# Bf16 instead of f32 integers in a SmoothQuant block: GpSimd clips in two passes and casts, TensorE transposes bf16, ScalarE copies without an offset

## The chip, the cores and the metric

One NeuronCore of a Trainium2 chip runs the whole kernel. The metric is the device time of one execution in microseconds. The kernel before takes 864.1 us (median of 3 runs, 863.93 to 864.49).

## The reference, cut to what matters

A decoder layer for 4 sequences of 512 tokens and 512 features: linear attention with 16 heads (x1 = layernorm(x + attention)), a quantised expert (x2 = layernorm(x1 + expert(x1))), and a gated FFN with 1408 hidden features and 4-bit weights (out = layernorm(x2 + ffn(x2))). The change lies in the expert, which calls this function twice, first with 512 input features (x and gate-up weights), then with 256 (the gated activation `a` and the down weights `v`):

```
def _smooth_quant_linear(x, w):
    ...                                   # s: per-feature smoothing from the column maxima
    xs = x / s
    ws = w * s
    x_scale = max(max|xs| over a row, EPS) / 127
    w_scale = max(max|ws| over a row, EPS) / 127
    x_q = jnp.clip(jnp.round(xs / x_scale), -127, 127)
    w_q = jnp.clip(jnp.round(ws / w_scale), -127, 127)
    return x_q @ w_q.T * x_scale * w_scale.T
```

## The kernel before, in words

Three phases follow one another, each a block in which every engine runs its own program and engines wait for each other through semaphores; a block ends when all its engines have ended.

1. `attention_phase` (0 to about 355 us): 16 chunks of 128 tokens. TensorE (PE) projects q, k and v with float32r matmuls, transposes q and k, forms scores and outputs. GpSimd (POOL) rotates q and k for the next chunk (L882 to L890), decays the state (L901, L910) and sums squares (L912, L914). ScalarE (ACT) and VectorE (DVE) drain PSUM. Beside the chunks, at places written out by hand in `EXPERT0_STEPS` as (chunk, part), run the steps of the expert for batch 0.
2. `weight_phase` (about 355 to 390 us): the 4-bit weights of the FFN are scaled into float32r.
3. `ffn_phase` (390 us to the end): for each of 4 batches, 11 hidden tiles of 128 features. A tile is on PE `hidden` for the gate (12 matmuls, L1476), `hidden` for up (12, L1476) and `down` of the tile before (12, L1486). After each of these three groups, at place 3*tile + 0, 1 or 2, PE runs the expert steps that `EXPERT_STEPS` puts there, for the next batch. ACT and DVE place their steps by the same table between their own parts of the tile; POOL has nothing else in this phase and runs the expert steps in order, as soon as their semaphores allow. Batches 1 to 3 of the expert run here, batch 3 of the FFN has none beside it.

The quantising of a matrix goes through these steps (names as in the two tables):

- `round_x`, `round_w`, `round_a`, `round_v` on ACT (L217): four instructions, one for each 128 rows, `src*inv + ROUND` with ROUND = 1.5 * 2^23, so that the f32 sum holds the rounded integer in its low bits. Each raises `rounded`.
- `clip_x`, `clip_w`, `clip_a`, `clip_v` on POOL (L279): two instructions, each for two of the four row blocks (128x1024 elements in the first layer, 128x512 in the second), min and max in one pass, in place, f32. Each raises `clipped`.
- `xq01`, `xq23`, `wq01`, `wq23`, `aq`, `vq` on PE (`quantised`, L467): for each of two feature blocks, four transposes of 128x128 f32 into one PSUM bank (6 or 7, in turn). The first feature block of a matrix waits for `clipped`, row blocks 0 and 1 for the first raise, 2 and 3 for the second. Before it writes a bank, PE waits until the bank's last user has drained it.
- the same names on ACT (`integers_out`, L223): the bank less ROUND, as bf16, into `q1T` or `q2T`.
- `w_scale`, `v_scale` (L456 on PE) broadcast a row of scales through the next bank; `products01` and so on (L476) multiply the bf16 integers; `rescale` (L392) on DVE; for the second layer `add` on POOL (L290), `sum` on DVE, `normalise` on ACT.

SyncE loads the next w once the bank of `vq1` is full, and the next v once that of `wq3` is full.

In PE's order an FFN batch has `xq01` at place 11, `xq23` 12, `wq01` 13, `wq23` 14, `w_scale` 15, then products, the second layer's columns at 19, rows at 21, `aq` 25, `vq` and `v_scale` 26, `y01` 27. In the attention, `xq01` and `xq23` are in chunk 8, `wq01` and `wq23` in chunk 9, `aq` and `vq` in chunk 14.

Of the kernel before, what the change touches and what calls it, by code (L numbers as in the profile page):

```python
# [7 lines left out]
ALU = mybir.AluOpType  # L8
# [142 lines left out]
class Expert:  # L151

    def __init__(self, nc, sem, memory):
# [4 lines left out]
            memory[n] for n in ("scale_row", "small", "e_stats", "e_mv", "biases"))  # L158
        self.v = self.w[:, :, 0:HALF]
        self.ps = memory["ps"]  # L160
        self.w_in, self.v_in, self.x1_in = sem("w_in"), sem("v_in"), sem("x1_in")
# [5 lines left out]
        self.inv_ready, self.rounded, self.clipped = sem("inv_ready"), sem("rounded"), sem("clipped")  # L167
        self.silu_g, self.e_var, self.e_root = sem("silu_g"), sem("e_var"), sem("e_root")
        self.gated, self.summed = sem("gated"), sem("summed")
        self.x2_shift, self.x2_done, self.mom = sem("x2_shift"), sem("x2_done"), sem("e_moments")  # L170
# [30 lines left out]
    def scalar_steps(self, act):  # L201
        nc, w, v, xb, act_s, q1T, q2T = self.nc, self.w, self.v, self.xb, self.act_s, self.q1T, self.q2T
        scale_row, small, mv = self.scale_row, self.small, self.mv
        ln_eps, plus_round, minus_round = (self.biases[:, n:n + 1] for n in (0, 2, 3))

# [14 lines left out]
        def integers_out(b, use, dst):  # L220

            self.wait_full(act, b, use)
            nc.scalar.activation(dst, self.bank(use)[:, :], ACT.Identity, bias=minus_round)\  # L223
                .then_inc(self.drain_sem(use), 1)
# [45 lines left out]
    def pool_steps(self, pool):  # L270
        nc, w, v, xb, act_s = self.nc, self.w, self.v, self.xb, self.act_s

        def clip(b, layer, weights):

            src = (v if layer else w) if weights else act_s
            width = HALF if layer else E
            for c in range(0, NC, 2):
                pool.wait_ge(self.rounded, (b * 4 + 2 * layer + weights) * NC + c + 2)
                nc.gpsimd.tensor_scalar(src[:, c:c + 2, 0:width], src[:, c:c + 2, 0:width], ROUND + QMAX,  # L279
                                        ROUND - QMAX, ALU.min, ALU.max).then_inc(self.clipped, 1)  # L280

# [158 lines left out]
    def tensor_steps(self, pe):  # L440
# [19 lines left out]
        def quantised(b, uses, src, count):  # L460
            for use in uses:
                k = int(use[2])
                filled = self.start_use(pe, b, use)
                for c in range(NC):
                    if k == 0:
                        pe.wait_ge(self.clipped, (b * 4 + count) * 2 + c // 2 + 1)
                    last = nc.tensor.transpose(self.bank(use)[:, c * P:(c + 1) * P], src[:, c, k * P:(k + 1) * P],  # L467
                                               ident)
                last.then_inc(filled, 1)
# [33 lines left out]
        def products_second(b):  # L503
# [16 lines left out]
            "aq": lambda b: quantised(b, ("aq0", "aq1"), act_s, 2),  # L520
            "vq": lambda b: quantised(b, ("vq0", "vq1"), v, 3),
            "v_scale": lambda b: rows_of(b, "v_scale", 10, NK, 4),
# [47 lines left out]
def attention_phase(nc, sem, a, memory, expert, x1):  # L570
# [5 lines left out]
    with ExitStack() as ctx:  # L576
# [197 lines left out]
        def _(act):  # L774
# [84 lines left out]
            act.wait_ge(ident_in, 16)  # L859
            nc.scalar.activation(ident16, ident, ACT.Copy).then_inc(ident16_set, 1)  # L860
            act.wait_ge(scale_ps, 2)
            nc.scalar.activation(scale_columns_of(shared), ps[6][:, 0:sum(SCALES)], ACT.Copy).then_inc(cols_set, 1)
# [172 lines left out]
        def _(pe):  # L1035
# [106 lines left out]
            for p in range(3):  # L1142
                pe.wait_ge(w_ready, (p + 1) * NK)
                project(0, p)
                if p == 1:
                    transpose_x(1)
            pe.wait_ge(ident16_set, 1)
            pe.wait_ge(scales_in, 32)
            at = 0
# [390 lines left out]
def build(nc, a, x1, x2, out):  # L1540
    with ExitStack() as ctx:
        def sem(name):
            return ctx.enter_context(nc.semaphore(name))
# [13 lines left out]
        memory["small"] = sb("small", [P, 16, NK])  # L1557
        memory["e_stats"], memory["e_mv"] = sb("e_stats", [P, NC, 6]), sb("e_mv", [P, 5, NC])
        memory["biases"] = sb("biases", [P, 4])
        memory["ps"] = [ctx.enter_context(nc.psum_tensor(f"ps{n}", [P, 512], F32)) for n in range(8)]  # L1560
# [36 lines left out]
```

## Time and profile before

| | |
|---|---|
| runs | 863.93, 864.1, 864.49 us |
| profiled execution | 866.59 us, of which the span of the trace is 864.8 us |
| PE | 746.2 us busy (86% of the span), mean granted clock 0.935 of 2.4 GHz |
| DVE, ACT, POOL | 459.4 us (53%), 361.1 us (42%), 212.4 us (25%) |
| DMA | 41.08 MB, mean 48 GB/s |

A row of a timeline reads: start in us from the span's start, duration in us from the first start to the last end of the merged instructions, engine, line, operation, output<-input tiles, shapes, xcount, and in brackets how long the engine had been idle just before, and who ended that. PE is pipelined: a matmul of 0.39 us starts 0.23 us after the one before it, so the pace of PE is the distance of starts, not the duration. PEld is the load of the stationary operand, which goes on beside the matmul before.

### The profile page before, as it was taken

The numbers are of one execution on the slowest core, as the hardware profiler recorded it, in microseconds if no ns is written. First come the engines' busy times: TensorE is split into PE (matmuls) and PEld (weight loads), VectorE is DVE, ScalarE is ACT, GpSimd is POOL, SyncE is SP. The second block draws the span as 40 slices with busy tenths as digits, with TensorE's granted clock in tenths as the row PEclk, the third lists the DMA queues.
The fourth block names the chain that finished last, engine by engine and source line by source line (L and its number), as shares of the span: only waits on it lengthen the run. The fifth ranks groups of instructions, "written<-read, shape, count | busy, mean of one in ns | idle before, by whom it ended". The sixth has DMA issues, their size and how long they took to land.

```text
span 864.8 us, 11954 instructions
## 1 busy us (share of the span) xinstructions
PE 746.2 (86%) x4662; PEld 602.7 (70%) x4662; DVE 459.4 (53%) x899; ACT 361.1 (42%) x583; POOL 212.4 (25%) x242
## 2 busy tenths in 40 slices
PE   4799989999997994268998987998997979999993
PEld 3688767878875783137876776876776858788882
DVE  3567566765655757376533457555446553432314
ACT  4244343455344362673432453532462634441212
POOL 0454344545433443490101210100300111200000
PEclk9899999999998998558998999998999999999997
DMA  8400100013001200401020120021120020100201
GB/s 304 171 14 13 38 13 13 2 49 122 14 17 43 77 2 1 146 1 49 1 74 1 49 97 1 1 74 49 49 97 0 24 97 1 38 12 1 98 0 49
DMA packets 25354, 41.08 MB, mean 48 GB/s; under 512 B 4954, under 2 KB 7642, under 8 KB 25178
## 3 DMA queue, kind: packets, MB, share of 16 engines
q1 hardware_dynamic: 23194, 37.27, 12.8%
q10 hardware_dynamic: 2112, 3.15, 1.1%
q8 instruction: 33, 0.54, 0.3%
q14 instruction: 15, 0.12, 0.0%
HBM read 28.88 MB, written 11.53 MB: 47 GB/s over the span
## 4 chain that ended last, share of the span: by engine, by line
PE 40%; DVE 7%; ACT 4%; issue 2%; POOL 1%; POOLq 0%; DVEq 0%; ACTq 0%
PE ps L1476 24%; PE ps L1486 11%; DVE act_s L317 2%; PE ps L467 2%; ACT h_hi L1317 1%; DVE silu L1409 1%; PE ps L476 1%; PE ps L448 1%; ACT silu L1334 1%; ACT xb L247 1%; PE ps L456 1%; DVE xc L1422 1%; POOL xb L290 1%; DVE w L317 1%; DVE h_lo L1393 1%
## 5 line engine op out<-in xcount | busy, mean ns | idle before, releaser
L1476 PE MATMUL ps<-x2T_lo,wgu_hi 128*128 128x512 f32 x352 | 140.9, 400 | 1.6 <-DVE x2T_lo L1399 1.6
L1476 PE MATMUL ps<-x2T_hi,wgu_hi 128*128 128x512 f32 x352 | 137.4, 390 | 0.0
L1476 PE MATMUL ps<-x2T_hi,wgu_lo 128*128 128x512 f32 x352 | 137.3, 390 | 0.0
L1409 DVE TENSOR_TENSOR silu<-ps,silu 128x512 f32<-128x512 f32 x44 | 30.4, 691 | 132.9 <-PE ps L1476 128.3
L1065 PE MATMUL ps<-wqkv_lo,xT_hi 128*128 128x512 f32 x192 | 82.0, 427 | 7.6 <-DVE wqkv_lo L945 4.0
L1486 PE MATMUL ps<-wdn_lo,h_hi 128*128 128x512 f32 x176 | 75.1, 427 | 4.9 <-DVE h_lo L1393 4.9
L1476 PEld LDWEIGHTS ps<-x2T_lo,wgu_hi 128*128 128x128 f32 x352 | 66.3, 188 | 15.9 <-DVE x2T_lo L1399 2.3
L1065 PE MATMUL ps<-wqkv_hi,xT_lo 128*128 128x512 f32 x192 | 77.2, 402 | 0.0
L1065 PE MATMUL ps<-wqkv_hi,xT_hi 128*128 128x512 f32 x192 | 77.1, 401 | 0.0
L882 POOL TENSOR_TENSOR rot<-qkv,tab 128x256 f32<-128x256 f32 x64 | 44.8, 732 | 128.7 <-ACT qkv L798 128.7
L1476 PEld LDWEIGHTS ps<-x2T_hi,wgu_lo 128*128 128x128 f32 x352 | 66.2, 188 | 14.2
L1476 PEld LDWEIGHTS ps<-x2T_hi,wgu_hi 128*128 128x128 f32 x352 | 66.3, 188 | 12.9
L1486 PE MATMUL ps<-wdn_hi,h_hi 128*128 128x512 f32 x176 | 71.7, 407 | 0.0
L1486 PE MATMUL ps<-wdn_hi,h_lo 128*128 128x512 f32 x176 | 71.5, 407 | 0.0
L1317 ACT ACTIVATE h_hi<-silu 128x512 fp32r<-128x512 f32 x44 | 27.6, 628 | 102.9 <-DVE silu L1409 102.9
L1323 ACT ACTIVATE silu<-ps 128x512 f32<-128x512 f32 x44 | 26.2, 595 | 93.3 <-PE ps L1476 93.2
L279 POOL TENSOR_SCALAR act_s<-act_s 128x1024 f32<-128x1024 f32 (+1 forms) x16 | 13.3, 829 | 201.4 <-ACT act_s L217 201.2
L996 DVE TENSOR_TENSOR masked<-ps,mask 128x512 f32<-128x512 f32 x64 | 39.7, 683 | 36.9 <-PE ps L1090 36.9
L1393 DVE TENSOR_TENSOR h_lo<-silu,h_hi 128x512 fp32r<-128x512 f32 x44 | 31.7, 721 | 45.7 <-ACT h_hi L1317 45.7
L798 ACT ACTIVATE qkv<-ps 128x512 f32<-128x512 f32 x48 | 28.6, 597 | 57.7 <-PE ps L1065 57.7
L1065 PEld LDWEIGHTS ps<-wqkv_lo,xT_hi 128*128 128x128 f32 x192 | 37.5, 195 | 18.5 <-DVE wqkv_lo L945 4.6
L1486 PEld LDWEIGHTS ps<-wdn_lo,h_hi 128*128 128x128 f32 x176 | 35.6, 202 | 13.8 <-DVE h_lo L1393 6.1
(168 smaller groups left out, 1512.2 us busy)
## 6 DMA issues: line engine op xcount, KB each, us to landing
x_in<-in_x_dram SPq DMA_DIRECT2D x16, 256.0 KB, 3.4
w<-in_fside_BxS2xS_dram SPq DMA_DIRECT2D x4, 1024.0 KB, 6.4
x_dram<-xb SPq DMA_DIRECT2D x4, 1024.0 KB, 4.5
xc<-x_dram SPq DMA_DIRECT2D x4, 1024.0 KB, 5.6
xb<-x_dram SPq DMA_DIRECT2D x3, 1024.0 KB, 5.5
out_dram<-xc SPq DMA_DIRECT2D x3, 1024.0 KB, 4.2
z<-in_x_dram SPq DMA_DIRECT2D x3, 768.0 KB, 4.6
x_dram<-z SPq DMA_DIRECT2D x3, 768.0 KB, 4.0
```

The source lines that it names most:

```text
L317: nc.vector.tensor_reduce(dst[:, columns], src[:, :, columns].rearrange("p c e -> p e c"), AX.X, ALU.max, apply_absolute_value=True).then_ ...
L467: last = nc.tensor.transpose(self.bank(use)[:, c * P:(c + 1) * P], src[:, c, k * P:(k + 1) * P], ident)
L798: nc.scalar.activation(qkv[:, n % 2, p * E:(p + 1) * E], bank(u, n)[:, :], ACT.Copy)\
L882: nc.gpsimd.tensor_tensor(rot[:, m], v, f, ALU.mult).then_inc(rot_a, 1)
L996: nc.vector.tensor_tensor(masked[:, j], in_groups(f"s{j}", n), mask[:, j], ALU.mult)\
L1065: last = nc.tensor.matmul(bank(u, n)[:, :], lhs, rhs, start=(k == 0 and m == 0), stop=(k == NK - 1 and m == 2))
L1317: nc.scalar.activation(h_hi[:, it % 2, :], silu[:, it % 2, :], ACT.Copy).then_inc(h_hi_done, 1)
L1323: nc.scalar.activation(silu[:, it % 2, :], ps[4][:, :], ACT.Silu).then_inc(silu_done, 1)
L1393: nc.vector.tensor_tensor(h_lo[:, it % 2, :], silu[:, it % 2, :], h_hi[:, it % 2, :].bitcast(F32), ALU.subtract).then_inc(h_lo_done, 1)
L1409: nc.vector.tensor_tensor(silu[:, it % 2, :], ps[5][:, :], silu[:, it % 2, :], ALU.mult)\
L1476: last = nc.tensor.matmul(dst[:, :], lhs, rhs, start=(k == 0 and n == 0), stop=(k == NK - 1 and n == 2))
L1486: last = nc.tensor.matmul(ps[c][:, :], lhs, rhs, start=(it == 0 and n == 0), stop=(it == NI - 1 and n == 2))
```

## The change: what it does

GpSimd's clip becomes two passes. The first takes the f32 value, subtracts ROUND, takes the minimum with 127 and writes bf16 into the lower half of the same row; the second, after a wait on the new semaphore `capped`, takes the maximum with -127 in place in bf16. The transposes read this bf16 matrix with a bf16 identity and write bf16 into the bank; ScalarE copies the bank's bf16 values without a bias. The identity `ident_bf16` is made by one more ScalarE instruction near the start, and PE waits for it once.

```
+        self.ident_bf16, self.ident_bf16_set = memory["ident_bf16"], sem("ident_bf16_set")
+        self.capped = sem("capped")
...
         def integers_out(b, use, dst):
             self.wait_full(act, b, use)
-            nc.scalar.activation(dst, self.bank(use)[:, :], ACT.Identity, bias=minus_round)\
+            nc.scalar.activation(dst, self.bank(use)[:, :].bitcast(BF16)[:, 0:E], ACT.Copy)\
                 .then_inc(self.drain_sem(use), 1)
...
         def clip(b, layer, weights):
-            src = (v if layer else w) if weights else act_s
+            src = w if weights else act_s
             width = HALF if layer else E
             for c in range(0, NC, 2):
                 pool.wait_ge(self.rounded, (b * 4 + 2 * layer + weights) * NC + c + 2)
-                nc.gpsimd.tensor_scalar(src[:, c:c + 2, 0:width], src[:, c:c + 2, 0:width], ROUND + QMAX,
-                                        ROUND - QMAX, ALU.min, ALU.max).then_inc(self.clipped, 1)
+                integers = src.bitcast(BF16)[:, c:c + 2, 0:width]
+                nc.gpsimd.tensor_scalar(integers, src[:, c:c + 2, 0:width], ROUND, QMAX, ALU.subtract, ALU.min)\
+                    .then_inc(self.capped, 1)
+                pool.wait_ge(self.capped, (b * 4 + 2 * layer + weights) * 2 + c // 2 + 1)
+                nc.gpsimd.tensor_scalar(integers, integers, -QMAX, None, ALU.max).then_inc(self.clipped, 1)
...
         def quantised(b, uses, src, count):
...
-                    last = nc.tensor.transpose(self.bank(use)[:, c * P:(c + 1) * P], src[:, c, k * P:(k + 1) * P],
-                                               ident)
+                    last = nc.tensor.transpose(self.bank(use)[:, :].bitcast(BF16)[:, c * P:(c + 1) * P],
+                                               src.bitcast(BF16)[:, c, k * P:(k + 1) * P], self.ident_bf16[:, :])
...
-            "vq": lambda b: quantised(b, ("vq0", "vq1"), v, 3),
+            "vq": lambda b: quantised(b, ("vq0", "vq1"), w, 3),
...
             nc.scalar.activation(ident16, ident, ACT.Copy).then_inc(ident16_set, 1)
+            nc.scalar.activation(expert.ident_bf16[:, :], ident, ACT.Copy).then_inc(expert.ident_bf16_set, 1)
...
             pe.wait_ge(ident16_set, 1)
+            pe.wait_ge(expert.ident_bf16_set, 1)
...
+        memory["ident_bf16"] = sb("ident_bf16", [P, P], BF16)
```

## Rows read from the trace of the kernel before

**Rows 1.** The page's first part: engine busy us (share of the span) xinstructions
```profile
PE 746.2 (86%) x4662; PEld 602.7 (70%) x4662; DVE 459.4 (53%) x899; ACT 361.1 (42%) x583; POOL 212.4 (25%) x242
```
**Rows 2.** The chain of waits, 425 to 455 us: start us, us, what
```profile
429.82 0.87 PE ps L467 x8
```
**Rows 3.** The chain of waits, 478 to 493 us
```profile
483.84 0.87 PE ps L467 x8
...
487.93 0.70 ACT q2T L223
```
**Rows 4.** Timeline of PE at `xq01` and after `vq`, both in the FFN
```profile
429.66 1.03 PE L467 MATMUL ps<-ident_ones,act_s 128*128 128x128 f32 x8
...
488.75 0.65 PE L456 MATMUL ps<-ident_ones,small 128*128 128x128 f32 x4 [0.41 <-ACT q2T L223]
```
**Rows 5.** Timeline of POOL: an own wait in chunk 7, the clips of one FFN batch
```profile
174.59 0.99 POOL L912 TENSOR_TENSOR sq<-sq 128x256 f32<-128x256 f32 x1 [1.74 <-ACT sq L839]
175.66 0.81 POOL L914 TENSOR_TENSOR sq<-sq 128x128 f32<-128x128 f32 x1
...
425.38 1.04 POOL L279 TENSOR_SCALAR act_s<-act_s 128x1024 f32<-128x1024 f32 x1 [37.93 <-ACT act_s L217]
426.79 1.04 POOL L279 TENSOR_SCALAR act_s<-act_s 128x1024 f32<-128x1024 f32 x1 [0.37 <-ACT act_s L217]
430.48 1.04 POOL L279 TENSOR_SCALAR w<-w 128x1024 f32<-128x1024 f32 x1 [2.65 <-ACT w L217]
...
482.04 0.61 POOL L279 TENSOR_SCALAR act_s<-act_s 128x512 f32<-128x512 f32 x1 [21.00 <-ACT act_s L217]
...
484.49 0.61 POOL L279 TENSOR_SCALAR w<-w 128x512 f32<-128x512 f32 x1 [0.85 <-ACT w L217]
```
**Rows 6.** Timeline of PE: short f32 and f16 matmuls, both at half clock
```profile
30.20 1.94 PE L1076 MATMUL ps<-ident_ones,qkv 128*128 128x128 f32 x8 [2.10 <-issue]
...
359.83 1.60 PE L1235 MATMUL ps<-scale_diag,shared 128*128 128x128 f16 x12 [18.55 <-POOL scale_diag L1198]
361.83 0.40 PE L1235 MATMUL ps<-scale_diag,shared 128*128 128x128 f16 x2 [0.39 <-POOL scale_diag L1198]
```
**Rows 7.** Groups by line and form: busy us, mean ns | idle before, releaser
```profile
L279 POOL TENSOR_SCALAR act_s<-act_s 128x1024 f32<-128x1024 f32 x8 | 8.4, 1044 | 134.5 <-ACT act_s L217 134.4
L279 POOL TENSOR_SCALAR act_s<-act_s 128x512 f32<-128x512 f32 x8 | 4.9, 615 | 66.9 <-ACT act_s L217 66.9
L1198 POOL TENSOR_TENSOR scale_diag<-ident_ones,shared 128x512 f16<-128x512 f32 x27 | 27.0, 1041 | 15.6 <-POOLq L576 15.6
L223 ACT ACTIVATE q2T<-ps,biases 128x512 bf16<-128x512 f32 x24 | 15.1, 680 | 10.5 <-PE ps L467 10.5
L228 ACT ACTIVATE scale_row<-ps 128x512 f32<-128x512 f32 x8 | 4.7, 592 | 0.8 <-PE ps L456 0.8
```
**Rows 8.** Timeline of DVE: one subtraction beside a clip, one alone
```profile
432.37 1.11 DVE L1393 TENSOR_TENSOR h_lo<-silu,h_hi 128x512 fp32r<-128x512 f32 x1 [2.94 <-ACT h_hi L1317]
...
438.59 0.69 DVE L1393 TENSOR_TENSOR h_lo<-silu,h_hi 128x512 fp32r<-128x512 f32 x1 [0.70 <-ACT h_hi L1317]
```
**Rows 9.** Timeline of the attention phase, chunk 8: a long wait of PE
```profile
195.44 0.50 PE L1130 MATMUL ps<-wo_lo,o_hi 128*128 128x512 f32 x1 [2.84 <-DVE o_lo L1008]
...
196.67 0.63 PE L1130 MATMUL ps<-wo_hi,o_hi 128*128 128x512 f32 x1
```
**Rows 10.** Timeline of chunk 9 (POOL) and chunk 14 (ACT)
```profile
201.23 1.04 POOL L279 TENSOR_SCALAR w<-w 128x1024 f32<-128x1024 f32 x1 [3.28 <-ACT w L217]
207.38 2.77 POOL L882 TENSOR_TENSOR rot<-qkv,tab 128x256 f32<-128x256 f32 x4 [2.57 <-ACT qkv L798]
...
321.77 1.24 ACT L223 ACTIVATE q2T<-ps,biases 128x512 bf16<-128x512 f32 x2
```
**Rows 11.** Timeline at the start: the last work before the first chunk
```profile
26.23 3.88 DVE L945 TENSOR_TENSOR wo_lo<-raw,wo_hi 128x512 fp32r<-128x512 f32 x4
28.14 0.28 ACT L862 ACTIVATE shared<-ps 128x132 f32<-128x132 f32 x1 [0.43 <-PE ps L1151]
```

More of the change, by code:

```diff
@@ L203, in scalar_steps @@
         scale_row, small, mv = self.scale_row, self.small, self.mv
-        ln_eps, plus_round, minus_round = (self.biases[:, n:n + 1] for n in (0, 2, 3))
+        ln_eps, plus_round = self.biases[:, 0:1], self.biases[:, 2:3]
         def smooth_root(b, layer):
```

## The prediction

> **What bounds the kernel now.** The engines' shares come first [rows 1]: PE is busy 86% of the span, no other engine above 53%. The chain of waits then says whether the edited steps lie on what sets the end. In the FFN they do: a block of eight f32 transposes is a link of the chain with 0.87 us of its own [rows 2]; there are four such links in each of batches 1 to 3, for `xq01`, `xq23`, `wq01` and `wq23`. In the second layer `aq` is such a link too, but of `vq` only the first half is: the chain goes from PE to ACT's q2T at 487.93 [rows 3], and PE's next instruction, the scale row at 488.75, stood 0.41 us for that drain [rows 4]. The timeline of POOL shows last where each clip stands before the transposes that read it [rows 5]: for `xq01` the second clip begins at 426.79 and ends 1.04 later, at 427.83, while PE starts at 429.66, a slack of 1.8 us. For `aq` the first clip begins at 482.04 and the second ends at about 483.6, and PE starts its block at 483.68 (483.84 by the chain, which shows every link 0.16 late, as 429.82 for 429.66). That slack is next to nothing. So the question is what PE gains per transpose against what longer clips lose in two places.
>
> **The transposes.** Today's pace is 0.87/8 = 0.109 us. The trace has no bf16 transpose. The nearest row is the f16 matmul of the same 128x128 shape: twelve take 1.60 us and two take 0.40, so one more costs 1.20/10 = 0.120. That is at half clock, where eight f32 transposes take 1.94 us, with the same tail of 0.28 a pace of 1.66/7 = 0.24 [rows 6]. So two-byte operands cost half, and at full clock 0.060. Eight then take 0.48: 0.39 us less a block. Bounds: no gain at all (if the f32 pace comes from something that bf16 keeps), and 0.43. I take 0.39, that of the f16 row.
>
> **The clips.** L279 costs 1.044 us for 1024 elements and 0.615 for 512, so 0.84 us per 1000 elements and 0.19 fixed [rows 7]. No row has a bf16 operand on POOL. A cast on the way out is in the trace: the tensor_tensor with f16 out takes 1.041 us for 512 elements [rows 7], with two inputs, and nothing marks its cast as dear. I take each of the two passes at today's duration, the row it is nearest to. Bounds for a pass: 0.6 of that (2-byte data moved twice as fast) and 1.7 times that (the two-input row, 1.041 against 0.615). An own wait between two POOL instructions costs 0.08: 174.59 + 0.99 = 175.58, next start 175.66 [rows 5]. Let r be the duration of a pass over today's.
>
> The Trainium skill, GPSIMD Engine Reference, section "Elementwise — side-by-side cycle accounting", says that a loop body of up to two ALU operations is bound by its read and write ports at about one cycle per element, and one of three or more by issue slots, about three operations a cycle. The trace agrees for the f32 clip with its two operations (0.84 us per 1000 elements is one cycle at the page's 1.2 GHz). Were unpacking and packing bf16 to make four operations of a pass, the page would give 1.33 cycles, an estimate of r = 1.27, and the sum below would come out at +0.3 us; this is the mechanism of the first rival.
>
> **`xq01` in the FFN.** POOL starts at 425.38 as now; four passes with three gaps of 0.08 end at 429.80. The second pair's rounding is ready at 426.79, so POOL never waits for ACT. PE reaches row block 2 at about 429.78 and can go on at 429.88 (0.08 for the semaphore). Six transposes (0.36) end at 430.24, against 430.53 now. Saves 0.29.
>
> **`xq23`, `wq01`, `wq23`.** 0.39 each. The w clip starts at 430.48 [rows 5] and ends 4.42 later, at 434.90; PE gets there two blocks and 24 matmuls after `xq01`, at about 437 less 0.7, covered by 1.4 us. The doubled POOL work lies beside DVE work: a DVE subtraction with two SBUF inputs took 1.11 us beside a clip and 0.69 without [rows 8]. Its result, h_lo, is wanted by a `down` one tile later, some 4 us on, so this costs nothing, and 0.4 each if that cover goes.
>
> The Trainium skill has this under GPSIMD Engine Reference, "Key points": GpSimd shares its SBUF interfaces with VectorE and contends with instructions that have two SBUF inputs. The trace agrees, DVE being the one that lost 0.42 us; were POOL's passes stretched too, r would rise, and some of the first rival's chance stands on that.
>
> **`aq`.** Four passes of 0.615 with three gaps from 482.04 end at 484.74, visible to PE at 484.82; six transposes end at 485.18. Now the block ends at 483.68 + 0.87 = 484.55. PE loses 0.63, with a new wait of about 1.0 us in it, and behind that wait stand all FFN matmuls of PE.
>
> **`vq` and `v_scale`.** The v clips follow on POOL without a pause (their rounding is ready at 484.49 [rows 5], before POOL is): 482.04 + 8*0.615 + 7*0.08 = 487.52. PE came to row block 0 about 0.63 before ACT's 487.93, at 487.30; it now comes to row block 2 at 487.30 + 0.63 + 0.12 = 488.05, a slack of 0.5. The first bank is full 4*0.049 = 0.20 sooner after the block's start. ACT's drain takes 680 ns on the mean with the bias, a copy of that size 592 [rows 7]: 0.09 less (bounds 0 and 0.3, should bf16 read faster from PSUM). So the scale row starts 0.63 - 0.20 - 0.09 = 0.34 later than now; the second half of `vq` is hidden behind the drain, before and after.
>
> An FFN batch: -0.29 - 3*0.39 + 0.34 = -1.12 us, three of them -3.4. After `vq` every wait (products, rescale, add, sums, normalise) starts from PE, so the difference passes on to the end. The DMA of v is issued when the bank of `wq3` is full and moves with it.
>
> **Attention, batch 0.** `xq01` in chunk 8 saves 0.39; its clips, from the end of POOL's sum of squares at 176.5 on, end by 181.0, and PE needs them after 183. `xq23` comes ahead of PE's wait of 2.84 us for o_lo [rows 9] and gives nothing. In chunk 9 `clip_w` runs from 201.23 to 205.65, and PE needs row block 2 after 206; the state decay (1.04) behind it on POOL ends at 206.8, and the rotation behind that waits for ACT until 207.38 in any case [rows 10], a cover of 0.5 us. So `wq01` and `wq23` save 0.78. In chunk 14 `aq` saves 0.39; `vq` is hidden behind ACT, whose two drains from 321.77 [rows 10] shrink by 2*0.09 = 0.18, which passes on to the next chunk's q and k. Sum -1.7 us; if other waits take it up, 0.
>
> **The rest.** The new identity costs ACT at most the 0.6 us of a copy of four times its size [rows 7], before the copy at 28.14 that PE needs; the first chunk waits for `wo_lo` until 26.23 + 3.88 = 30.11 [rows 11], so over 1 us of cover is left.
>
> **Sum.** -3.4 - 1.7 = -5.1 us. The profiled execution, 866.59 us with a span of 864.8, would take 861.5. The median of the runs is 2.5 us below the profiled execution; 864.1 becomes 859.0.
>
> **With other r.** A batch loses 4.18*(r - 1) at `xq01` and 2.46*(r - 1) at `aq`, so the sum is -5.1 + 19.9*(r - 1), zero at r = 1.26. Beyond that the slacks at `vq` (0.5) and in chunk 9 (0.5) are used up: at r = 1.5 they add 3*0.7 and about 1.7, and the sum is +8.7.
>
> **Rivals.**
> 1. *bf16 passes are dearer on POOL*: PE waits for the clips at `xq01` and `aq`. For it: no row shows bf16 on POOL. Against: the f16 row shows no price for a cast. It decides from r = 1.26; at r = 1.5 the time is 872.8. Slower by over 0.2% has a chance of 0.20 by this; the band of r from 1.15 to 1.33, 862 to 866 us, has 0.15.
> 2. *The new wait at `aq` costs PE its clock.* After the wait of 2.84 us in chunk 8 eight matmuls last 0.63 instead of 0.40 [rows 9], 1.6 us lost and more. Against: the wait of 0.41 after `vq` left the matmuls behind it alone, and 1.0 lies nearer to it. In three batches +4.8, so 863.8. Chance 0.08.
> 3. *bf16 transposes keep the pace of 0.109.* A batch then gains nothing at four blocks, loses 0.92 at `aq` and regains 0.09: +2.5 in all, 0.2 back in the attention, 866.4. For it: their source lies in rows of 2048 bytes, and loading the stationary side may set the pace. Against: the f16 row. Chance 0.07.
>
> **Chances.** The forecast, r up to 1.15, has 0.50. Faster by over 0.2%, about what a measurement of this kernel can tell from no change: 0.57 (the forecast and 0.07 of the others); within 0.2%: 0.18; slower: 0.25. The forecast's own range is 856 (r = 0.85) to 862. For 8 in 10 the range goes on to 872, nearly the first rival at r = 1.5.
>
> **What would show it.** L467 at a pace of 0.055 to 0.065 in PE's timeline; POOL's 64 clip instructions with means near 1.04 and 0.61; in each FFN batch a wait of PE for POOL of about 1.0 us at `aq` and 0.1 at `xq01`; L223 near 592 ns; PE's mean clock as before. A pass over 1.3 us for 1024 elements would make the prediction wrong, and so would matmuls of 0.63 behind each `aq`.

## The result, and the profile after

The changed kernel takes 963.2 us (median of 4 runs, 959.32 to 965.12) against 864.3 us (863.93 to 865.97) for the kernel before in the same session: a ratio of 1.113, 95% interval 1.110 to 1.117. Slower by 11%; 859.0 was predicted, and the range ended at 872. The profiled execution took 963.76 us, with a span of 962.0 us and a mean granted clock of 0.901 (before 0.935).

The page's first part for the kernel after answers to [rows 1]:

```profile
PE 763.9 (79%) x4662; PEld 609.8 (63%) x4662; DVE 460.0 (48%) x899; ACT 358.5 (37%) x584; POOL 342.4 (36%) x274
```

POOL has 32 instructions more and is busy 130.0 us more. PE has the same 4662 instructions and is busy 17.7 us more, so of the 97.2 us by which the span grew, 79.5 are new idle time of PE. The groups by form show the cause (busy us, mean ns | idle before). L282 is the first pass, L285 the second, L225 ScalarE's copy; they answer to [rows 7].

```profile
L282 POOL TENSOR_SCALAR act_s<-act_s 128x1024 bf16<-128x1024 f32 x8 | 29.1, 3638 | 134.3 <-ACT act_s L219 133.9
L285 POOL TENSOR_SCALAR act_s<-act_s 128x1024 bf16<-128x1024 bf16 x8 | 22.2, 2773 | 0.7
L282 POOL TENSOR_SCALAR act_s<-act_s 128x512 bf16<-128x512 f32 x8 | 15.4, 1928 | 63.8 <-ACT act_s L219 63.5
L285 POOL TENSOR_SCALAR act_s<-act_s 128x512 bf16<-128x512 bf16 x8 | 11.9, 1492 | 0.7
...
L225 ACT ACTIVATE q1T<-ps 128x512 bf16<-128x512 bf16 x24 | 13.0, 594 | 35.8 <-PE ps L472 35.8
```

A clip of 128x1024 was one instruction of 1.044 us. It is now a pass of 3.64 and one of 2.77, 6.41 us together: in the prediction's terms r is 3.1 for 1024 elements and 2.8 for 512. The chain of waits in the first FFN batch now goes through POOL without a break (start us, us, what):

```profile
450.30 0.81 ACT act_s L219
...
451.19 3.65 POOL act_s L282
454.83 0.07 issue
454.90 2.77 POOL act_s L285
...
457.76 3.64 POOL act_s L282
...
474.61 2.78 POOL w L285
...
477.44 0.82 PE ps L472 x6
```

PE's timeline for the same stretch shows who stands behind it; before, the first of these blocks was one row without a wait [rows 4].

```profile
457.82 0.37 PE L472 MATMUL ps<-ident_bf,act_s 128*128 128x128 bf16 x2 [2.21 <-POOL act_s L285]
464.30 0.82 PE L472 MATMUL ps<-ident_bf,act_s 128*128 128x128 bf16 x6 [6.11 <-POOL act_s L285]
...
465.45 0.63 PE L1483 MATMUL ps<-x2T_hi,wgu_hi 128*128 128x512 f32 x1
...
469.12 0.62 PE L472 MATMUL ps<-ident_bf,act_s 128*128 128x128 bf16 x8
...
477.44 0.82 PE L472 MATMUL ps<-ident_bf,w 128*128 128x128 bf16 x6 [4.78 <-POOL w L285]
```

The reader is to see three things. The waits are at `xq01` and `wq01`, which need all four row blocks, and not at `xq23`. After a wait the FFN matmuls take 0.63 us (465.45) instead of 0.39 for some six of them, at the lower clock level (the granted clock is 0.50 from 464.3 to 467.5 us and 1.00 from 468.6 on): part of the 17.7 us of extra busy time. And the transposes did get shorter: eight that nothing holds up take 0.62 us, not 1.03 [rows 4]. In the second layer of this batch PE stands 1.77 and 3.30 us at `aq` and 2.36 at `vq`. Over the whole execution PE waits (us in total, times, longest):

```profile
PE ps L472 <- POOL act_s L285: 48.9, 14, 6.3
PE ps L472 <- POOL w L285: 29.0, 8, 6.2
```

That is 77.9 of the 79.5 us of new idle time. By stage (us, PE busy, PEld, DVE, ACT, POOL busy, clock, DMA share, GB/s), first the kernel before, its attention and its FFN:

```profile
0.00:360.00 360.00, 300.20 (x2572) 246.33 (x2573) 215.12 (x470) 156.18 (x244) 142.72 (x175) 0.94 0.17 57
...
390.00:864.80 474.80, 426.66 (x1960) 344.67 (x1959) 222.52 (x394) 182.70 (x290) 42.20 (x39) 0.96 0.11 39
```

and the kernel after:

```profile
0.00:386.00 386.00, 308.14 (x2575) 252.01 (x2576) 215.01 (x470) 155.59 (x245) 174.97 (x183) 0.91 0.16 53
...
416.00:962.00 546.00, 436.39 (x1959) 346.09 (x1957) 223.24 (x394) 180.69 (x290) 140.25 (x63) 0.92 0.10 34
```

The attention with its part of the expert grew by 26 us, the FFN by 71.2, which is 23.7 for each of the three batches that have an expert beside them. POOL's surplus is 32.5 us a batch, so about three quarters of it reached the end.

### The profile page after: what moved, and what is told of

Same layout as the page of the kernel before. It is cut to its first block, busy times and chain, and to the rows that moved or that the text cites. A ratio compares the mean times of both kernels' runs of the same rounds, so it can differ in the third digit from the quotient of the medians.

```text
span 962.0 us, 11987 instructions
## 1 busy us (share of the span) xinstructions
PE 763.9 (79%) x4662; PEld 609.8 (63%) x4662; DVE 460.0 (48%) x899; ACT 358.5 (37%) x584; POOL 342.4 (36%) x274
## 3 DMA queue, kind: packets, MB, share of 16 engines
q10 hardware_dynamic: 2112, 3.15, 0.9%
## 4 chain that ended last, share of the span: by engine, by line
PE 28%; POOL 13%; DVE 8%; ACT 4%; issue 3%; DVEq 0%; POOLq 0%; ACTq 0%
PE ps L1483 17%; PE ps L1493 7%; POOL act_s L282 3%; POOL w L282 3%; POOL w L285 3%; POOL act_s L285 3%; DVE act_s L322 2%; ACT h_hi L1324 1%; DVE silu L1416 1%; PE ps L453 1%; PE ps L481 1%; DVE small L361 1%; ACT silu L1341 1%; ACT xb L249 1%; PE ps L461 1%
## 5 line engine op out<-in xcount | busy, mean ns | idle before, releaser
L282 POOL TENSOR_SCALAR act_s<-act_s 128x1024 bf16<-128x1024 f32 (+1 forms) x16 | 44.5, 2783 | 198.0 <-ACT act_s L219 197.3
L1493 PE MATMUL ps<-wdn_lo,h_hi 128*128 128x512 f32 x176 | 78.8, 448 | 4.9 <-DVE h_lo L1400 4.9
L1493 PE MATMUL ps<-wdn_hi,h_hi 128*128 128x512 f32 x176 | 74.7, 424 | 0.0
L1493 PE MATMUL ps<-wdn_hi,h_lo 128*128 128x512 f32 x176 | 73.5, 417 | 0.0
L1324 ACT ACTIVATE h_hi<-silu 128x512 fp32r<-128x512 f32 x44 | 27.6, 628 | 102.3 <-DVE silu L1416 102.3
L1071 PEld LDWEIGHTS ps<-wqkv_lo,xT_hi 128*128 128x128 f32 x192 | 38.1, 198 | 19.9 <-DVE wqkv_lo L951 5.0
L472 PE MATMUL ps<-ident_bf,act_s 128*128 128x128 bf16 x96 | 11.1, 261 | 48.9 <-POOL act_s L285 48.9
```

Source lines behind the costliest of these rows:

```text
L282: nc.gpsimd.tensor_scalar(integers, src[:, c:c + 2, 0:width], ROUND, QMAX, ALU.subtract, ALU.min)\
L1071: last = nc.tensor.matmul(bank(u, n)[:, :], lhs, rhs, start=(k == 0 and m == 0), stop=(k == NK - 1 and m == 2))
L1324: nc.scalar.activation(h_hi[:, it % 2, :], silu[:, it % 2, :], ACT.Copy).then_inc(h_hi_done, 1)
L1493: last = nc.tensor.matmul(ps[c][:, :], lhs, rhs, start=(it == 0 and n == 0), stop=(it == NI - 1 and n == 2))
```

## The experiments

The theory: the cost is POOL's alone. What in POOL's passes is dear can be the bf16 operands or the cast (theory A of the first expectation), input and output in the same row (B), or the operations themselves (C). Rivals to the theory are that the wait on `capped` costs the time, or that the transposes and ScalarE's copy cost something too.

**1. Fifteen forms of POOL instruction by themselves.** The kernel before, and behind POOL's last step 45 more instructions, each form three times, each waiting for the one before it.

```
+            for _ in range(3):
+                then(nc.gpsimd.tensor_scalar(w32, a32, 3.0, None, ALU.max))             # L1405
+            for _ in range(3):
+                then(nc.gpsimd.tensor_scalar(w32, a32, 3.0, 5.0, ALU.subtract, ALU.min)) # L1407
...
+                then(nc.gpsimd.tensor_scalar(w16, a32, 3.0, 5.0, ALU.subtract, ALU.min)) # L1411
...
+                then(nc.gpsimd.tensor_scalar(w16, a16, 3.0, None, ALU.max))             # L1415
...
+                then(nc.gpsimd.tensor_scalar(w16, a16, 3.0, 5.0, ALU.min, ALU.max))     # L1417
...
+                then(nc.gpsimd.tensor_scalar(w32, a16, 3.0, None, ALU.max))             # L1421
...
+                then(nc.gpsimd.tensor_tensor(w32, a32, a32, ALU.add))                   # L1429
...
+                then(nc.gpsimd.tensor_tensor(w16, a16, a16, ALU.add))                   # L1433
```

> The kernel before, with 45 more GpSimd instructions after the last expert step, while GpSimd is otherwise idle: fifteen forms, three times each, all on 128x1024 elements in two row blocks as in the clip (one form on 1024 elements in one row), each with a wait for the one before. Theory A (a bf16 operand takes a pass off the rate of one element per 0.84 ns, whatever the operation and place): f32 to f32 about 1.04 us with one or two operations, f32 to bf16 3.6 us with two operations, in place or not, bf16 to bf16 2.8 us. Rival B (it is the place: input and output overlap in the same row): out of place the bf16 forms take about 1.04 us. Rival C (it is the operation: subtract with min, or a single max with no second operation): the f32 to f32 forms with these operations take 2.8 to 3.6 us, and the bf16 form with min and max 1.04. Among the bf16 forms, one operation less should save about 0.85 us if operations are counted (3.64 against 2.77 us in the changed kernel).

It took 868.32 us in one execution, its extra work partly behind the rest. The groups by form:

```profile
L1405 POOL TENSOR_SCALAR w<-act_s 128x1024 f32<-128x1024 f32 x3 | 8.3, 2769 | 0.3
L1407 POOL TENSOR_SCALAR w<-act_s 128x1024 f32<-128x1024 f32 x3 | 10.9, 3636 | 0.2
...
L1411 POOL TENSOR_SCALAR w<-act_s 128x1024 bf16<-128x1024 f32 x3 | 10.9, 3630 | 0.2
...
L1417 POOL TENSOR_SCALAR w<-act_s 128x1024 bf16<-128x1024 bf16 x3 | 3.1, 1041 | 0.2
...
L1421 POOL TENSOR_SCALAR w<-act_s 128x1024 f32<-128x1024 bf16 x3 | 8.3, 2771 | 0.2
...
L1429 POOL TENSOR_TENSOR w<-act_s 128x1024 f32<-128x1024 f32 x3 | 5.7, 1894 | 0.2
L1433 POOL TENSOR_TENSOR w<-act_s 128x1024 bf16<-128x1024 bf16 x3 | 5.7, 1893 | 0.2
```

A single `max` costs 2769 ns from f32 to f32 and 2771 from bf16 to f32; the pair (subtract, min) costs 3636 with f32 out and 3630 with bf16 out; the pair (min, max) costs 1041 in bf16, as it did in f32. The type of the operands and the cast cost next to nothing (a lone `max` from bf16 to bf16 has a mean of 2837 out of place and 2798 in place), and the operations decide: C holds, A and B do not. The two durations of the changed kernel, 3638 and 2773, are those of (subtract, min) and of a lone `max`.

**2. Fifteen more pairs of operations**, all from f32 to bf16, in the same way.

```
-                then(nc.gpsimd.tensor_scalar(w32, a32, 3.0, None, ALU.max))
+                then(nc.gpsimd.tensor_scalar(w16, a32, 3.0, None, ALU.mult))            # L1405
...
+                then(nc.gpsimd.tensor_scalar(w16, a32, 3.0, 5.0, ALU.max, ALU.min))     # L1413
...
+                then(nc.gpsimd.tensor_scalar(w16, a32, 3.0, 5.0, ALU.mult, ALU.add))    # L1419
...
+                then(nc.gpsimd.tensor_scalar(w16, a32, 3.0, 5.0, ALU.add, ALU.min))     # L1427
```

> As e1_pool_forms, with fifteen other pairs of operations, all f32 in and bf16 out, out of place, 128x1024. Theory C2 (after e1_pool_forms: GpSimd has a fast loop for certain pairs of operations, min then max being one, and a slow general one at 2.5 ns per element for one operation and 3.3 for two): most pairs take 3.6 us, most single operations 2.8, and a few pairs 1.04. Rival C3 (the general loop is slow only where max or subtract is the operation, because they are written with a compare or a call): single mult, add and the pair mult, add take 1.04 to 1.9 us. The order matters under C2: max then min could be slow although min then max is fast.

One execution took 892.92 us. The groups by form:

```profile
L1413 POOL TENSOR_SCALAR w<-act_s 128x1024 bf16<-128x1024 f32 x3 | 10.9, 3625 | 0.2
L1405 POOL TENSOR_SCALAR w<-act_s 128x1024 bf16<-128x1024 f32 x3 | 8.3, 2774 | 0.3
L1419 POOL TENSOR_SCALAR w<-act_s 128x1024 bf16<-128x1024 f32 x3 | 3.1, 1045 | 0.2
```

Every lone operation (max, min, add, subtract, multiply) took 2767 to 2774 ns. With (subtract, min) of experiment 1, ten pairs took 3.6 to 3.7 us: (subtract, min), (max, min), (min, min), (max, max), (subtract, mult), (subtract, max), (add, min), (mult, min), (add, add), (subtract, add). Three did not: (min, max) at 1041 in experiment 1, (mult, add) at 1045, and (add, mult) at 1150 over three (the shortest took 1044). The order counts: (max, min) is 3.5 times as dear as (min, max). The kernel before happened to use a fast pair.

**3. The clip alone, in f32.** The kernel before with its one clip taken apart into `min` and `max`, with the new wait; transposes and copy as before.

```
-                nc.gpsimd.tensor_scalar(src[:, c:c + 2, 0:width], src[:, c:c + 2, 0:width], ROUND + QMAX,
-                                        ROUND - QMAX, ALU.min, ALU.max).then_inc(self.clipped, 1)
+                block = src[:, c:c + 2, 0:width]
+                nc.gpsimd.tensor_scalar(block, block, ROUND + QMAX, None, ALU.min).then_inc(self.capped, 1)
+                pool.wait_ge(self.capped, (b * 4 + 2 * layer + weights) * 2 + c // 2 + 1)
+                nc.gpsimd.tensor_scalar(block, block, ROUND - QMAX, None, ALU.max).then_inc(self.clipped, 1)
```

> The kernel before, whose clip is done in two f32 passes (min, then max, with the wait between them); transposes and ScalarE as before. Theory A (only bf16 is dear): each pass about 1.04 and 0.61 us, PE waits about 0.2 us longer at xq01 and 1.0 at aq in the FFN; since nothing is saved on PE, a batch loses about 0.1 at xq01, 0.9 to 1.0 at aq and vq: +3 us, 867. Rival C (a pass of one operation is slow): passes of 2.8 us and more, and 940 us or more.

940.8 us (939.25 to 945.23), a ratio of 1.089 (1.085 to 1.092). Nothing on POOL and no transpose is in bf16 in this kernel, and 76 of the 99 us of the loss are there. Its wait row, with passes of 2772 and 2769 ns:

```profile
PE ps L470 <- POOL act_s L283: 37.4, 14, 5.3
```

**4. The transposes and the copy alone.** To have bf16 transposes with POOL's clip untouched, ROUND becomes 1.5 * 2^23 + 2^14, so that the lower two bytes of the f32 value are the integer plus 2^14; PE transposes these halves as bf16 (every second element), and ScalarE reads the bank as int16 and takes 2^14 off.

```
+LOW = 2.0 ** 14
+ROUND = 1.5 * 2.0 ** 23 + LOW
...
+            nc.scalar.activation(dst, self.bank(use)[:, :].bitcast(I16)[:, 0:E], ACT.Identity, bias=minus_low)\
...
+                    last = nc.tensor.transpose(self.bank(use)[:, :].bitcast(BF16)[:, c * P:(c + 1) * P],
+                                               src.bitcast(BF16)[:, c, 2 * k * P:2 * (k + 1) * P:2], self.ident_bf16[:, :])
```

> As e3_low_half_two_f32 but with the one f32 pass of the kernel before on GpSimd: bf16 transposes alone. Theory A: no wait at xq01 and aq, PE saves 0.39 us a block; FFN batch -5*0.39 - 0.3 at vq = -2.2, three -6.7, attention -1.7: -8.4 us, 856. Rival D: 862 or more.

861.07 us (860.08 to 861.86), 0.996 (0.994 to 0.997) of the kernel before. With POOL left alone the transposes give a gain, but 3.7 us of the 8.4 expected. In the trace the FFN is 4.0 us shorter where 6.7 were expected: `xq23` gains 0.02 us a batch instead of 0.39, because PE there stands for ScalarE's drain of the bank. The attention gains 0.9 from its first output to its last, where 1.7 were expected. A block that nothing holds up:

```profile
427.42 0.62 PE L471 MATMUL ps<-ident_bf,act_s 128*128 128x128 bf16 x8
```

The next matmul starts 0.43 us after such a block's start, after 0.79 before.

**5. Both sides crossed: the transposes of 4 with the two f32 passes of 3.**

> The changed kernel with r = 1: two f32 passes on GpSimd, bf16 transposes on PE. The rounding adds 2^14 more, so that the lower 16 bits of each f32 are the integer plus 16384, which read as bf16 is a number between 1 and 4; PE transposes these halves (every second bf16 of a row) and ScalarE reads the bank as int16 and takes 16384 off. Theory A: this is the kernel that was forecast, 859 us. Rival D (the transposes themselves or the clock at the new waits carry part of the 99 us): 865 or more. If the stride of two elements slows the load of the stationary operand, L472 paces above 0.065 us and the time is 862 to 866.

938.75 us, 1.086 (1.084 to 1.088), 2 us below experiment 3, with intervals that overlap. The passes decide; what the transposes give beside them is not clear of noise here.

**6. The same with the fast pair twice.** Both passes of 5 become (min, max), each about 1.045 us.

```
-                nc.gpsimd.tensor_scalar(block, block, ROUND + QMAX, None, ALU.min).then_inc(self.capped, 1)
+                nc.gpsimd.tensor_scalar(block, block, ROUND + QMAX, ROUND - QMAX, ALU.min, ALU.max).then_inc(self.capped, 1)
...
-                nc.gpsimd.tensor_scalar(block, block, ROUND - QMAX, None, ALU.max).then_inc(self.clipped, 1)
+                nc.gpsimd.tensor_scalar(block, block, ROUND + QMAX, ROUND - QMAX, ALU.min, ALU.max).then_inc(self.clipped, 1)
```

> e3_low_half_two_f32 with the fused min and max in each of the two passes (the second has nothing left to clip): two passes of 1.04 and 0.61 us, which is r = 1 of the forecast, and bf16 transposes. Theory A2 (the forecast failed only in the duration of the passes): 859.0 us as forecast, and against e4_low_half (861.1, no second pass) 3 to 4 us more or less than that: waits of PE of 0.1 us at xq01 and 1.0 us at aq in each FFN batch. As e4_low_half saved 3.6 us where the same working gives 8.4, this one may lie at 864. Rival: the second pass costs more than its waits (clock), 868 or more.

866.22 us (862.09 to 867.79), 1.0005 (0.9988 to 1.0022). With the number of instructions, the wait and the transposes of 5, 72.5 us are gone. What is left also says that a second pass at today's price eats what the transposes give.

**7. The changed kernel with its second pass made a fast pair.**

```
-                nc.gpsimd.tensor_scalar(integers, integers, -QMAX, None, ALU.max).then_inc(self.clipped, 1)
+                nc.gpsimd.tensor_scalar(integers, integers, QMAX, -QMAX, ALU.min, ALU.max).then_inc(self.clipped, 1)
```

> The changed kernel with its second pass written as min with 127 and max with -127 (the min has nothing left to do), everything else as in the changed kernel. If the pair of operations alone sets the rate, each second pass takes 1.04 and 0.61 us in place of 2.77 and 1.49, and the PE waits at xq01 shrink by 2*1.73 = 3.5 us, at wq01 by up to 3.5, at aq and vq by 0.88 each pass, 3.5 in all: about 10 us a batch, 40 us in all, 923 us. If bf16 input in place had a price of its own: above 940.

918.89 us, 1.062 (1.059 to 1.064): 44 us less for more arithmetic in the instruction.

**8. The kernel that the prediction had in mind.** In addition the first pass as (add, mult by 1.0), a fast pair, so that each of the two passes costs what the one clip did.

```
-                nc.gpsimd.tensor_scalar(integers, src[:, c:c + 2, 0:width], ROUND, QMAX, ALU.subtract, ALU.min)\
+                nc.gpsimd.tensor_scalar(integers, src[:, c:c + 2, 0:width], -ROUND, 1.0, ALU.add, ALU.mult)\
```

> The changed kernel with both passes written as pairs that e1_pool_forms and e5_pool_forms2 showed fast: add -ROUND then mult by 1.0 into bf16, and min with 127 then max with -127 in bf16. Everything else is the changed kernel; it is the kernel that was forecast, with r = 1. Theory C2 (the pair of operations sets GpSimd's rate): passes 1.04 and 0.61 us; by the forecast's own working 859.0 us, by e6_low_half_two_fast (866.2, with a ScalarE drain 0.09 us dearer) 865. Rival A (bf16 in place has a price in this place): above 880.

866.44 us (865.17 to 867.25) against 865.79, 1.0006 (0.9997 to 1.0015). So 97 of the 99 us come from the choice of operations in the two passes. The two passes over 1024 elements cost 2.09 us together here, 4.67 in 7 and 6.41 in the changed kernel, and the times 866.4, 918.9 and 963.2 rise by 20 and then by 25 us for each us of that cost (experiment 5, with 5.54 and 938.8, lies between the last two). Counted out, a batch has four such pairs of passes over 1024 elements, and four over 512 whose cost grows half as much ((3.42 - 1.23)/(6.41 - 2.09) = 0.51). That makes 6.0 us a batch for each us, and 24 for four batches: once the covers are used up, about all that is added to POOL's passes reaches the end.

But at r = 1 the forecast was -5.1 us, and this kernel gains nothing. Its trace is read below, and the next two runs test that reading.

**9. One pass, with bf16 transposes and the plain copy.** POOL reads the lower halves of the rounded values as int16, clips with the fast pair, and writes bf16.

```
-                nc.gpsimd.tensor_scalar(src[:, c:c + 2, 0:width], src[:, c:c + 2, 0:width], ROUND + QMAX,
-                                        ROUND - QMAX, ALU.min, ALU.max).then_inc(self.clipped, 1)
+                nc.gpsimd.tensor_scalar(src.bitcast(BF16)[:, c:c + 2, 0:width],
+                                        src.bitcast(I16)[:, c:c + 2, 0:2 * width:2], QMAX, -QMAX,
+                                        ALU.min, ALU.max).then_inc(self.clipped, 1)
```

> One GpSimd pass as before and bf16 transposes: the clip reads the lower 16 bits of each f32 (1.5*2^23 + n) as int16, which is n, takes min with 127 and max with -127 and writes bf16 packed into the row; ScalarE copies without an offset. If the pair of operations sets the rate also for int16 with a stride of two, the pass takes 1.04 and 0.61 us, and the time is that of e4_low_half (861.1) less 0.09 us for each drain on the path: 860 to 861. If the stride or int16 costs a general loop: passes of 1.5 us or more and 868 or more.

```profile
L282 POOL TENSOR_SCALAR act_s<-act_s 128x1024 bf16<-128x1024 int16 x8 | 8.3, 1037 | 135.5 <-ACT act_s L220 135.5
```

860.41 us (855.88 to 861.02), 0.994 (0.993 to 0.996) of the kernel before: faster than both kernels, and the lowest median of all, though its interval overlaps that of experiment 4. Everything that the change meant to bring is in it, with one clip at the old price (1037 ns).

**10. The second pass of `v` in chunk 14 left out.** In experiment 8 the attention came out longer, not shorter. Chunk 14 shows how. DVE's four pairs of 16-bit instructions (before L932 and L935, here L938 and L941) go out from 317.45 to 318.67 before, each 0.22 long:

```profile
317.59 0.22 DVE L935 TENSOR_SCALAR sign<-halves 128x264 uint16<-128x264 uint16 x1
```

In experiment 8 they take from 316.57 to 319.83:

```profile
316.81 1.34 DVE L941 TENSOR_SCALAR sign<-halves 128x264 uint16<-128x264 uint16 x1
318.07 0.77 DVE L938 TENSOR_SCALAR magnitude<-halves 128x264 uint16<-128x264 uint16 x1
...
318.90 0.48 DVE L938 TENSOR_SCALAR magnitude<-halves 128x264 uint16<-128x264 uint16 x1
...
319.83 0.71 DVE L944 TENSOR_TENSOR magnitude<-magnitude,sign 128x1056 uint16<-128x1056 uint16 x1
```

POOL in the same stretch has been pushed back by its two extra passes, so that the state's addition, which before ran from 315.96 to 317.25 and so largely ahead of them, now lies on them:

```profile
316.19 0.61 POOL L285 TENSOR_SCALAR w<-w 128x512 bf16<-128x512 bf16 x1
316.77 1.29 POOL L916 TENSOR_TENSOR kv<-kv,kv_old 128x512 f32<-128x512 f32 x1
318.02 0.74 POOL L918 TENSOR_TENSOR sq<-sq 128x256 f32<-128x256 f32 x1
318.83 0.46 POOL L920 TENSOR_TENSOR sq<-sq 128x128 f32<-128x128 f32 x1
```

DVE's instruction of 1.34 us ends at 318.15, POOL's L916 at 318.06; the next of 0.77 ends at 318.84, L918 at 318.76; the one of 0.48 ends at 319.38, L920 at 319.29. On ACT the packing (L811) waits for DVE and stands ahead of the drains of `vq`, and PE's scale row stands behind these (before: 322.49, a wait of 0.83):

```profile
323.09 0.65 PE L461 MATMUL ps<-ident_ones,small 128*128 128x128 f32 x4 [2.76 <-ACT q2T L225]
...
327.64 0.45 PE L1096 MATMUL ps<-qT_hi,kT_hi 32*128 32x128 f32 x4
```

L1096, 0.31 us long before, is 0.45 behind that wait. The experiment takes only the second pass of `v` away, in this batch alone.

```
+                one_pass = turn == 3
...
+                if one_pass:
+                    continue
```

> The kernel of two fast passes, with the second pass of v left out in batch 0 alone (chunk 14 of the attention; v is then not clipped there, the order of POOL's other work is as it was). Theory 'DVE held up by POOL': in chunk 14 the second pass pushes POOL's work onto DVE's eight 16-bit instructions (L938 and L941), which took 3.26 us from start to last end instead of 1.22 (one of them 1.34 us instead of 0.22); ACT's packing and its drains of vq came that much later, and PE stood 2.8 us at v_scale instead of 0.8 and lost its clock behind it. Expected: DVE's eight back to about 1.2 us, the wait at v_scale 0.8 to 1.3 us, the matmuls L1096 behind it at full pace, attention 2 to 3 us shorter, so 863.5 us (862.5 to 865). Rival 'the loss is chance': the stretch at half clock falls elsewhere in each kernel, and the time stays at 866 to 867.

862.9 us, 0.9967 (0.9951 to 0.9984), against 1.0006 for experiment 8: two instructions of 0.61 us were worth 3.4 us by these ratios (2.4 by the medians). In the trace the last output of the attention comes 3.15 us earlier than in experiment 8.

```profile
321.56 0.65 PE L465 MATMUL ps<-ident_ones,small 128*128 128x128 f32 x4 [1.18 <-ACT q2T L225]
...
325.85 0.33 PE L1100 MATMUL ps<-qT_lo,kT_hi 32*128 32x128 f32 x4 [1.90 <-DVE qdT L996]
```

DVE's eight are back at 0.22 each, from 316.64 on, the wait at 1.18, and the matmuls behind it at 0.31. That the loss in this chunk was chance is excluded, and the chain through DVE is what the trace shows; but this experiment takes the pass away together with DVE's delay, so it does not separate the two. The next one does.

**11. The same work, `clip_v` of that batch behind the sums of squares.**

```
-                 "round_v": (14, 0), "aq": (14, 0), "clip_v": (14, 1), "vq": (14, 2), "v_scale": (14, 2),
+                 "round_v": (14, 0), "aq": (14, 0), "clip_v": (14, 2), "vq": (14, 2), "v_scale": (14, 2),
```

> The kernel of two fast passes, with all of its work, and clip_v of batch 0 moved on POOL from place (14, 1) to (14, 2), behind the sums of squares. Theory 'DVE held up by POOL': DVE's eight 16-bit instructions run between POOL's other work in 1.2 to 1.5 us, ACT's packing starts at about 319 as in the kernel before, less the lead of 0.9; the v passes end at about 321.3, PE's vq waits some 1 to 1.5 us for them, behind which ACT's packing (2 us) still runs in any case, so v_scale waits no more than before and the attention is 1 to 2 us shorter than with clip_v at (14, 1): 865 us (864 to 866). Rival 'PE pays for the later clip': vq's wait costs PE its clock as the 2.8 us did, and nothing is gained: 866 to 868.

865.79 us (861.75 to 867.92), 1.0009 (0.9996 to 1.0021): nothing gained over experiment 8. DVE's instructions are at 0.22 again, but PE pays at `vq`:

```profile
318.19 0.27 PE L472 MATMUL ps<-ident_bf,w 128*128 128x128 bf16 x2 [0.93 <-POOL w L285]
319.49 0.74 PE L472 MATMUL ps<-ident_bf,w 128*128 128x128 bf16 x6 [1.03 <-POOL w L285]
...
326.69 0.48 PE L1096 MATMUL ps<-qT_hi,kT_lo 32*128 32x128 f32 x4
```

and its matmuls run at the lower clock level behind it (the granted clock is 0.54 from 326 to 332 us), as the rival had it. From the chunk's output to the next, this order loses 3.8 us on the kernel before, that of experiment 8 loses 2.8. So a DVE without delay does not save the time as long as the second pass is there. Neither of the two places tried for it in this chunk is free; in 9, where it is gone, nothing has to be placed.

## Why the prediction was wrong, step by step

- **The clips, the step that failed.** "I take each of the two passes at today's duration, the row it is nearest to." The row was nearest in shape and type, and neither sets the price: the pair of operations does. Passes of 3.64 and 2.77 us instead of 1.04 (r = 3.1) lie far outside the bounds of 0.6 and 1.7, because one bound was a guess about 2-byte data and the other the row of a two-input instruction, and none came from a row with another pair of operations. [Rows 7] held only one tensor_scalar of POOL, the clip with (min, max) itself; that the new passes use (subtract, min) and a lone `max` should have made its price no evidence for them.
- **Where it strikes.** The first rival had the places right (`xq01`, `aq`, then `vq` and chunk 9) but not the size, nor a reason for more than r = 1.5, and it tied the dearness to bf16, which experiment 3 excludes. At r = 3 its formula gives -5.1 + 19.9*2 = 35 us, before the used-up slacks at `vq` and in chunk 9 (3.8 us at r = 1.5); 99 were measured. `wq01` in the FFN (4.78 us in the first batch) and `xq01` in the attention (5.70), both hidden at r = 1, have no term in it, and the waits at `vq` (2.36) and in chunk 9 (2.08 and 6.21) grow with r as well.
- **The Trainium skill's rule.** The prediction cited GPSIMD Engine Reference, "Elementwise — side-by-side cycle accounting", for about one cycle per element up to two ALU operations. The runs differ: a lone operation takes (2770 - 1490)/512 = 2.5 ns per element, a general pair (3638 - 1928)/512 = 3.3, and only the fast pairs 0.83. The measurement decides.
- **The transposes: right.** Eight take 0.62 us instead of 1.03, a pace near 0.06 as predicted, and a link of the chain is 0.46 to 0.47 us after 0.87. By the start of the next matmul the gain is 0.36 a block (0.79 to 0.43), where 0.39 was taken from the chain.
- **ScalarE's drain: right.** 594 ns, predicted 592. The identity's copy is hidden, as said.
- **`xq01` and `aq` at r = 1 (experiment 8): right.** `xq01` gains 0.28 (predicted 0.29). At `aq`:

```profile
483.41 0.28 PE L472 MATMUL ps<-ident_bf,act_s 128*128 128x128 bf16 x2
484.54 0.51 PE L472 MATMUL ps<-ident_bf,act_s 128*128 128x128 bf16 x6 [0.85 <-POOL act_s L285]
484.86 0.47 PE L1493 MATMUL ps<-wdn_lo,h_hi 128*128 128x512 f32 x1
...
488.87 0.65 PE L461 MATMUL ps<-ident_ones,small 128*128 128x128 f32 x4 [0.54 <-ACT q2T L225]
```

  The next matmul comes 1.45 after the start instead of 0.79, a loss of 0.66 (predicted 0.63), and the scale row 5.46 after it instead of 5.07, 0.39 later (predicted 0.34). The second rival did not happen: the matmul behind that wait is 0.47 long, as behind any block.
- **`xq23`: half right.** It gains 0.20, not 0.39. PE now comes to the banks before ScalarE has drained them (the weight loads of experiment 8):

```profile
435.38 0.23 PEld L472 LDWEIGHTS ps<-ident_bf,act_s 128*128 128x128 bf16 x4 [0.17 <-ACT q1T L225]
```

  ScalarE first rounds w (its L219, 430.92 to 433.86) and writes `h_hi` (L1324, 433.75 to 434.37), which the faster transposes do not hasten. A batch at r = 1 is then -0.28 - 0.20 - 2*0.36 + 0.39 = -0.8 us instead of -1.12, three of them -2.4; from the first FFN tile to the last the trace shows -2.0.
- **Attention at r = 1: wrong in sign.** Predicted -1.7. In the trace of experiment 8 the last output of the attention comes 1.9 us later than before, though the first one came 1.05 earlier. The outputs of chunks 9 to 12 gain 1.0 us on that of chunk 7 (predicted 1.2). In chunk 13 the trace loses 1.6 us to the clock (0.83 from 280 to 290 us, 1.00 before), behind the same wait of 1.77 us as before. Experiment 11, whose work is the same up to chunk 14, kept 1.00 there and lost nothing, so the edit does not force this loss; what brings it on stays open. In chunk 14 it loses 2.8 by experiment 10's mechanism: the prediction took `vq` as hidden behind ScalarE's drains, and did not follow what the extra passes push back on POOL itself, onto DVE's 16-bit instructions, ACT's packing and the very drains that were to hide it.
- **The sum at r = 1: wrong.** 859.0 was predicted, and experiment 8 took 866.4 against 865.8 before: +0.6 instead of -5.1. Against 9, on one chip, the second pass costs 6.0 us. Chunk 14 is 2.4 to 3.4 of it, and `aq` 0.9 in each of three batches (5.46 in experiment 8 from `aq` to the scale row, 4.53 in experiment 4 with one pass) is 2.8. So even with passes at the assumed price the forecast would have missed.

## What to carry to other kernels

Price an instruction by its operations, not only by its shape and types: where the trace has no row with the same operation pair on that engine, the range is open until one is measured, and one probe of fifteen forms behind the kernel's last step does it. Splitting a fused clip made each pass over 1024 elements 2.7 to 3.5 times as dear as the whole here, so a cast is better folded into the fused pass (int16 view in, bf16 out) than added as a pass. And where an engine with slack of its own gets longer work, follow what is queued behind that work on it: it may land on another engine's short instructions.

## What the runs showed of the hardware

- GpSimd's tensor_scalar on 128x1024: 1.04 us for (min, max), (mult, add), (add, mult) and a plain f32-to-bf16 copy (1037 to 1047, but for one of three that took 1360 to 1383 in three of the forms), 2.77 for any lone operation, 3.6 to 3.7 for ten other pairs; within 3% the same for f32, f16 and bf16, in place or not (as far as tried), and 1037 ns with every second int16 as input. tensor_tensor add is 1.89 in f32 and in bf16. A second operation that does nothing useful (mult by 1.0 behind an add, a `min` with a bound never reached ahead of the `max`) makes the instruction 2.6 times as fast.
- A VectorE instruction on 16-bit data with one input, 0.22 us by itself, took 1.34, 0.77 and 0.48 us beside GpSimd's tensor_tensor and ended 0.08 to 0.09 us after it. The Trainium skill, GPSIMD Engine Reference, "Key points", names the shared SBUF interfaces, with contention for VectorE instructions in a 2-port perf mode or with two SBUF inputs. The ones held here have a single input, so only the first of the two would fit them; no run here shows in which mode they ran.
- Who was held differed with the order. In the kernel before, VectorE's row of these instructions was under way at 318.25 when GpSimd's L912 began, and there GpSimd's was the longer (0.99 us against 0.74 in experiment 8) and VectorE's kept their 0.22. VectorE's tensor_tensor at 318.67 also ran beside L912, so which of its instructions made L912 longer is not shown, nor was the order varied by itself.
